# Counting edges per node: a loop of comparisons and matmuls written out for all hundred groups, its line numbers compared in four pieces, with four buffers in place of two

## The reference, cut to what matters

```
x = _layernorm(x + _L0_gnn_ref(x, edge_attr_48, src, dst, L0_gnn_eps), axis=-1)
x = _layernorm(x + _L1_gnn_ref(x, edge_weight, src, dst), axis=-1)
x = _layernorm(x + _L2_gnn_ref(x, edge_weight1, L2_gnn_weight1, L2_gnn_weight2, L2_gnn_bias1, L2_gnn_bias2, src, dst, edge_type_8), axis=-1)
x = _layernorm(x + _L3_gnn_ref(x, L3_gnn_theta_w, L3_gnn_theta_b, L3_gnn_phi_w, L3_gnn_phi_b, src, dst), axis=-1)
```

## Time and profile before

| | us |
|---|---|
| median of 3 runs | 4202.54 |
| lowest and highest of them | 4201.44, 4211.9 |
| span of the profiled execution | 5230.0 |
| counting stage in it, first compare to last result | 51.7 to 416.1 |

### The profile page before, as it was taken

How to read it: one execution, slowest core, us unless ns; L and a number is a source line. 1 busy time by engine, 2 the same in 40 slices (tenths; PEclk the granted TensorE clock), 3 DMA queues, 4 the chain that set the end, 5 groups by cost and what they waited for, 6 DMA issues and landing times. The chain is left out here.

```text
span 5230.0 us, 57991 instructions
## 1 busy us (share of the span) xinstructions
PE 2653.0 (51%) x9282; PEld 1302.4 (25%) x9282; DVE 2825.2 (54%) x7308; ACT 1341.5 (26%) x4703; POOL 2738.0 (52%) x2688
## 2 busy tenths in 40 slices
PE   1270000566666665357543577767666103975543
PEld 0150000232222233112111234433333001332222
DVE  3298998566666454356432366656665223652322
ACT  0003333344333232112111233333332011431111
POOL 4406773554454455544365355555556555646565
PEclk7695555777777777678776688877887556995555
DMA  7705777555555442334422544444443243321111
GB/s 249 295 0 164 217 216 198 140 146 144 140 142 134 141 115 78 86 99 114 93 55 52 123 116 113 110 102 106 101 102 77 64 125 91 73 63 31 30 30 22
DMA packets 513328, 587.96 MB, mean 112 GB/s; under 512 B 222598, under 2 KB 402382, under 8 KB 508182
## 3 DMA queue, kind: packets, MB, share of 16 engines
q1 hardware_dynamic: 365050, 417.75, 26.1%
q0 software_dynamic: 92160, 94.65, 11.9%
q10 hardware_dynamic: 55972, 74.03, 4.4%
HBM read 289.08 MB, written 303.60 MB: 113 GB/s over the span
## 5 line engine op out<-in xcount | busy, mean ns | idle before, releaser
L508 POOL DMA_INDIRECT xdst<-in_x,dstc x400 | 447.1, 1118 | 385.0 <-PEq L667 198.6
L284 POOL DMA_INDIRECT gb<-nodes,ib x400 | 386.1, 965 | 460.4 <-ACT ib L873 338.5
L268 PE MATMUL bank<-ident,act 128*99 128x128 f32 x400 | 87.4, 357 | 642.5 <-issue 570.5
L278 PE MATMUL bank<-ident,scan 99*128 99x99 f32 (+2 forms) x1120 | 205.6, 313 | 376.8 <-DVE scan L1032 139.8
L1314 PE MATMUL bank<-e_bxT,w 105*128 105x512 f32 x432 | 252.9, 702 | 224.7 <-ACT e_hm L1233 173.1
L304 PE MATMUL bank<-chosen,rec 128*6 128x512 bf16 x1200 | 360.8, 464 | 1.1 <-ACT packed L901 0.8
L1265 POOL DMA_INDIRECT out<-e_xob,e_ob x288 | 295.5, 1026 | 101.3 <-issue 86.8
L278 PEld LDWEIGHTS bank<-ident,scan 99*128 99x128 f32 (+2 forms) x1120 | 159.3, 213 | 560.5 <-issue 559.8
L284 POOL DMA_INDIRECT ugb<-nodes,ib x160 | 170.0, 1062 | 240.5 <-ACT ib L1984 158.5
L586 PE MATMUL bank<-hot_at,hot_no 128*125 128x400 f16 x800 | 167.9, 357 | 235.1 <-DVE hot_at L612 138.0
L284 POOL DMA_INDIRECT parent<-upper_rows,ib x160 | 159.3, 996 | 197.1 <-ACT ib L1544 148.2
(11 more groups left out here) (332 smaller groups left out, 7175.9 us busy)
## 6 DMA issues: line engine op xcount, KB each, us to landing
nodes<-wt SPq DMA_DIRECT2D x40, 1286.2 KB
lone_rows<-gb ACTq DMA_DIRECT2D x100, 294.0 KB
e_lsb<-lone_rows SPq DMA_DIRECT2D x72, 294.0 KB
parents<-zeros SPq DMA_DIRECT2D x21, 960.0 KB
upper_rows<-tb SPq DMA_DIRECT2D x100, 194.0 KB
deep_sum<-zeros SPq DMA_DIRECT2D x20, 960.0 KB
layer<-zeros SPq DMA_DIRECT2D x20, 960.0 KB
kb<-edge_keep SPq DMA_DIRECT2D x100, 192.0 KB
```

The source lines that it names most:

```text
L268: last = nc.tensor.transpose(slot(dst_ps[0:w, :], t), rows_sb[:, t, c0:c0 + w], ident[:, :])
L278: last = nc.tensor.transpose(dst_ps[:, t, 0:w], slot(cols_sb[0:w, :], t), ident[0:w, 0:w])
L284: yield nc.gpsimd.indirect_dma_start(out=dst[s][:, t, 0:width], out_offset=None, in_=table, in_offset=bass.IndirectOffsetOnAxis(ap=ib[s][: ...
L508: nc.gpsimd.indirect_dma_start(out=xdst[:, k * F:(k + 1) * F], out_offset=None, in_=a["x"], in_offset=bass.IndirectOffsetOnAxis(ap=dstc[:, ...
```

## The change

In `compare`, the one `tensor_tensor` over 512 columns becomes four `tensor_scalar` over 128 columns, each with its line number read per partition, and they alternate with the four of `hot_at`. Both read their number straight from `line_no` and `line_at`. The tile `marks`, ACT's copies and the semaphore `s_mark` go. The loops of DVE and PE are written out for all hundred groups, with constants in the place of registers. There are AHEAD = 4 buffers of the one-hots in place of two; the compare of group g now waits for PE to be through with group g - 4.

```diff
@@ buffers @@
-            hot_no = [sc(f"hot_no{b}", [P, T, P], F16) for b in range(2)]
-            hot_at = [sc(f"hot_at{b}", [P, T, LINE], F16) for b in range(2)]
-            marks = [sc(f"marks{b}", [P, T]) for b in range(2)]
+            hot_no = [sc(f"hot_no{b}", [P, T, P], F16) for b in range(AHEAD)]
+            hot_at = [sc(f"hot_at{b}", [P, T, LINE], F16) for b in range(AHEAD)]
@@ scalar @@
-                    def mark(i, b):
-                        g = i * 2 + b
-                        wait(act, s_hots, g - 1)
-                        nc.scalar.copy(marks[b][:, :], col(line_at, g)).then_inc(s_mark, 1)
...
@@ tensor @@
-                    def add(i, b, first=False, final=False):
-                        pe.wait_ge(s_hots, i * 2 + b + 1)
+                    def add(g, first=False, final=False):
+                        b = g % AHEAD
+                        pe.wait_ge(s_hots, g + 1)
                         pe.sem_inc(pe_turn, 1)
...
-                    with pe.Fori(1, NG // 2 - 1) as i:
-                        for b in range(2):
-                            add(i, b)
...
+                    for g in range(NG):
+                        add(g, first=g == 0, final=g == NG - 1)
@@ vector @@
-                    def compare(i, b):
-                        g = i * 2 + b
-                        wait(dve, s_count, g - 1)
-                        nc.vector.tensor_tensor(hot_no[b][:, :, :], steps_h[:, 0:P].unsqueeze(1).to_broadcast([P, T, P]), col(line_no, g).unsqueeze(2).to_broadcast([P, T, P]), ALU.is_equal)
-                        dve.wait_ge(s_mark, g + 1)
+                    def compare(g):
+                        b = g % AHEAD
+                        wait(dve, s_count, g - AHEAD + 1)
                         for t in range(T):
-                            last = nc.vector.tensor_scalar(hot_at[b][:, t, :], steps_h[:, :], marks[b][:, t:t + 1], None, ALU.is_equal)
+                            k = g * T + t
+                            nc.vector.tensor_scalar(hot_no[b][:, t, :], steps_h[:, 0:P], line_no[:, k:k + 1], None, ALU.is_equal)
+                            last = nc.vector.tensor_scalar(hot_at[b][:, t, :], steps_h[:, :], line_at[:, k:k + 1], None, ALU.is_equal)
                         last.then_inc(s_hots, 1)
...
-                    with dve.Fori(2, NG // 2) as i:
-                        for b in range(2):
-                            compare(i, b)
+                    for g in range(NG):
+                        compare(g)
```

More of the change, by code:

```diff
@@ L31 @@
 EARLY = 32
+AHEAD = 4
 FIRST = 7
@@ L526, in gnn @@
             s_fixed, s_term = scope.sem("h_fixed"), scope.sem("h_term")
-            s_zeros, s_fill, s_list, s_ends, s_endc, s_mark, s_hots, s_count, s_upto, s_below, s_fin, s_turn = (
-                scope.sem(f"h_{n}") for n in ("zeros", "fill", "list", "ends", "endc", "mark", "hots", "count", "upto",
+            s_zeros, s_fill, s_list, s_ends, s_endc, s_hots, s_count, s_upto, s_below, s_fin, s_turn = (
+                scope.sem(f"h_{n}") for n in ("zeros", "fill", "list", "ends", "endc", "hots", "count", "upto",
                                               "below", "fin", "turn"))
@@ L564, in _ @@
                 def _(act):
-                    def mark(i, b):
-                        g = i * 2 + b
-                        wait(act, s_hots, g - 1)
-                        nc.scalar.copy(marks[b][:, :], col(line_at, g)).then_inc(s_mark, 1)
-                    for i in range(2):
-                        for b in range(2):
-                            mark(i, b)
-                    with act.Fori(2, NG // 2) as i:
-                        for b in range(2):
-                            mark(i, b)
                     act.wait_ge(s_endc, 16)
@@ L588, in add @@
                         last.then_inc(s_count, 1)
-                    add(0, 0, first=True)
-                    add(0, 1)
-                    with pe.Fori(1, NG // 2 - 1) as i:
-                        for b in range(2):
-                            add(i, b)
-                    add(NG // 2 - 1, 0)
-                    add(NG // 2 - 1, 1, final=True)
+                    for g in range(NG):
+                        add(g, first=g == 0, final=g == NG - 1)
                     pe.wait_ge(s_upto, 2)
```

## The result

The changed kernel takes 4217.1 us (median of 5 runs, 4213.82 to 4220.78), the kernel before 4202.54 (4200.3 to 4211.9). The ratio is 1.003 with a 95% interval of 1.0017 to 1.0043: slower by 7 to 18 us, which lies around the bound that I had set for what a measurement can tell from no change. The forecast was 4208.0.

A forecast was written before the change was run, and what follows sets the result against it. The prediction took DVE to bound the counting stage, at 1.95 us a group without late increments. Short comparisons add 5.5 us, copies, loops and four buffers nothing: 4202.5 + 5.5 = 4208.0 us, range 4150 to 4255.

The forecast's parts named there:

- within 0.3%: Whole kernel: a time of 4190 to 4215 us, about what a measurement can't tell from no change; chance 0.65.
- main term: DVE's counting stage: four short comparisons for one wide add 0.055 us a group, +5.5 us over a hundred groups.
- late increments: DVE's waits for PE's semaphore in the counting stage, 152.9 us: taken for a cost of profiling, absent from timed runs.
- B: Counting stage: stalls real, from loops or register waits; vanishing gives 4054 us (0.06), two cases within 0.3% have 0.07.
- The line numbers: DVE's comparisons: 0.167 us for each of 128 columns, so 2.01 us a group for 1.95.
- bounds of -22 and +31 us: Short comparisons on DVE: -22 us if their fixed part were half as long, +31 if not overlapped at all.
- Rival D: POOL's gathers lengthened by DVE's comparisons, 1.89 for 0.94 us: slower, 4279 us; chance 0.03.
- The copies: ACT's hundred copies of 0.19 us lie wholly under DVE's compares: removing them gains nothing.
- The loops: DVE's and PE's loops: removing branch and registers gives nothing where DVE is the bound; gain 0.
- rival C: Written out code fetched while fills own the DMA engines: six holes on DVE, 46 us, 4254 us; chance 0.09.
- rival A: Counting stage: increments late by a small L without profiler too; four buffers cover about 4.3 us; 4157 us, chance 0.13.
- Four buffers: One-hot buffers between DVE and PE: nothing gained, as PE is 0.3 us early already with two.

The follow-up runs named there:

- pe_loop: The kernel after, with PE's code a loop of four groups again; DVE stays written out, with four pieces and four buffers: 4216.04 us (1.0029).
- loop_wide_dve_out: Against the kernel before: DVE written out, no number copies, four buffers; PE in a loop, one wide comparison of 512 columns: 4203.52 us (0.9998).
- loop_pieces: The kernel before, loops and two buffers kept, line numbers compared in four pieces of 128 columns and copied by ACT too: 4212.35 us (1.0018).
- two_slots: The kernel after, with two buffers in place of four: 4230.57 us (1.0067).
- one_wide: The kernel after, with the line numbers compared by one instruction of 512 columns as before: 4209.76 us (1.0013).
- act_half: From the kernel before: loops of four groups, four buffers, ACT makes two of four `hot_no` columns, DVE compares the other two: 4171.1 us (0.9925).

## Why the prediction was right, and where it was wrong

The time came out 9 us above the forecast, inside the range of 4150 to 4255. The forecast's own range, 4199 to 4213, to which I had given 0.58, it misses by 4 us, and the median lies 2 us above the end of the case "within 0.3%" (4215), while the ratio, 1.003 with 1.0017 to 1.0043, leaves both sides of that bound open. The mechanism of the main term was right. But of 11.7 us of stage I had seen 5.5. That the rest is so small is in part luck: with two buffers PE's holes take 19 us, the four buffers hold back 15 of them, and I had worked out neither number.

| part | forecast | by the stage | from |
|---|---|---|---|
| pieces, start-up | +5.5 | +5 | 2.00 against 1.95 us, no gathers |
| pieces, beside POOL's gathers | 0 | +3.6 to +4.1 | pe_loop, loop_wide_dve_out, loop_pieces |
| PE written out | 0 | +3.7 | after less pe_loop |
| DVE written out, copies gone, four buffers | 0 | -1.1 | loop_wide_dve_out less before |
| together | +5.5 | +11.7 | after less before |

**Whether the late increments exist without the profiler.** Right, and everything hung on it. I had forecast a stage from 51.7 us to 247 for the last compare and a tail of 15 us; the kernel before, run again, has its last comparison at 250.3 (a group takes 1.98 us and not 1.95 beside POOL). Of the reasons, the balance of 1027.5 us between span and median was sound. The cause that I named, the recording of PE's many instructions, was not shown: nine further profiled executions, with the same 9282 matmuls and mostly the same fills, have no such wait. I had taken a mishap of one execution for a property of profiling, and so forecast "the same gaps" and a span of 5230 for the profile after. That was wrong. So was the test that I set myself: "if those gaps are gone from the profile, B holds and I am wrong by 150 us". They are gone, and B (loops or register waits cause them) is false, since they are gone from the unchanged kernel too. A test on the changed kernel alone could not tell these apart.

**The line numbers.** The line through the 800 and 512 columns gave 0.167 us from start to start and 2.01 us a group; measured are 0.16 and 2.00. (4 x 0.167 less 0.61 is 0.058 and not 0.055, so by its own numbers the sum was +5.8.) The bounds of -22 and +31 us were not needed. What failed is the step from the group to the hundred: both durations came from stretches in which POOL gathers nothing (beside the rows from 961.57 to 962.62 it waits for ACT until 962.63), and I used them for a stage of which four fifths run beside 128 gathers. Rival D looked at this same encounter from POOL's side only, and gave little to it, rightly: POOL's gathers are not long enough to matter. The price was on DVE's side, 0.05 us for each gather where it had been 0.02.

The start-up of some 158 cycles of the Trainium skill ("VectorE: DVE Perf Modes", section "Side-by-side"), with which I had worked out +9 us, comes close to the total of the pieces (8.6 and 9.1) by accident: the part without gathers is 5.

**The copies.** Right, zero: with them and without, DVE stands for nothing (loop_pieces, pe_loop).

**The loops.** On DVE right, zero both ways. On PE wrong. I had the case in rival C, with its sign to be seen in the profile ("gaps in the middle of a group, before an instruction with no wait"), and that is what stands there. But I priced it for DVE, where there is no such hole, with POOL's hole of 7.59 us as the price, and waved PE's away: "a hole in PE's code would be bridged by four buffers". Bridged it was, by three quarters. What was missing is the lead to weigh a hole against. I had written that the wait for PE "is met 6 us ahead". In the kernel after PE is through with one group at 137.40 us and the comparison that needs its buffer starts at 141.85: 4.45 us ahead, close to the 4.3 that I had given for L in rival A. The hole of 4.4 us and the matmuls at the lower clock behind it make the group in which they stand 5.7 us late, so the buffers don't cover it, and some 1.3 us a hole reach DVE. PE then makes up its arrears with 0.46 us a group. Measured: 3.7 us for three long holes and a short one, and 15.4 more with two buffers.

POOL's hole of 7.59 us, my price for C, stands in the kernel before and after at the same gather; it has to do with neither of the parts that are changed. With the fills later it stands behind the same gather, the 113th, but is 3.30 us long, so full DMA engines lengthen it too; they run at full strength in the eight other profiled executions, where it is 7.3 to 8.2 us. What it is stays open.

**Four buffers.** "Nothing" was right for the stage as I saw it (1.1 us at its start, no more), and wrong for the kernel that they came with, where they hold back 15 us. The slack with two buffers, "0.3 us", is 301.57 - 301.40 = 0.17 us by the earlier trace rows; that changes nothing here.

**A, B and D.** A would have shown a median of 4140 to 4185: in the nine other profiled executions no comparison waits for a late increment. B in all its forms falls with it. D's deciding point was 1.63 us for each gather; they take 1.28 with their issue.

The unit in which code comes is told by the queue: five packets of 16 KB in this stage, one for fifteen groups of PE (the rows under pe_loop). In "Runtime: NRT & Kernel Launch", section "Instruction fetch mechanics", the Trainium skill gives blocks of 256 instructions as the unit of fetching, and holds the cost of crossing into the next to be mostly hidden. The unit agrees: a group of PE is 8 weight loads, 8 matmuls and one increment, 17 instructions, so that 256 hold 120.5 matmuls, and the holes stand 121, 120 and 121 matmuls apart. The cost does not: with the DMA engines at 403 GB/s one block in fifteen groups held PE for 4.3 to 4.5 us, with them at 20 GB/s for 0.7 to 0.9. And a loop, which it would have avoided, cost nothing here.

## What to carry to other kernels

Before anything rests on a wait that makes one profiled execution much longer than the timed runs, take the profile of the unchanged kernel again: it cost one run and would have replaced the most uncertain argument of this prediction. Writing out a loop makes its code a DMA transfer, which here came late when the DMA engines were full; leave PE in its loop there, and count the slower matmuls behind a hole with the hole. DVE written out cost nothing. Before trusting buffers to bridge a hole, take the lead that they give from the rows (4.45 us) and compare it with the whole delay of the group (5.7). And where DVE is the bound, cutting one instruction into four paid start-up four times, and more for each encounter with POOL; moving half of it to an idle engine gained 30.4 us of stage where the whole change had lost 11.7.

## What the runs showed of the hardware that I had not expected

- Increments of semaphores behind PE's work came up to 40 us late in one profiled execution (span 5230.0 us), and in none of nine others, eight of which had the fills at 403 to 404 GB/s where it had 402. The cause was not found.
- PE's code arrives in packets of 16 KB, one for fifteen groups of this stage. Four of the five in it go with a hole of PE's, and PE goes on 2.2 to 2.5 us behind the packet (2.8 once, in two_slots). The holes are 4.3 to 5.3 us long with full DMA engines (after, two_slots, one_wide) and 0.7 to 0.9 with nearly idle ones. DVE's code arrives in 8 KB packets and delays nothing that shows, under the same load.
- Behind a hole of 4.4 us PE's granted clock was 0.50 and a matmul of 400 columns took 0.35 us, against 0.19 ahead of it. Behind a hole of 0.9 us the granted clock was 1.00 and a matmul took 0.18.
- An indirect DMA issued by POOL costs DVE about 0.02 us in the kernel before, 0.05 us where half of DVE's instructions are short, and nothing in act_half; POOL's gathers start every 1.32, 1.28 and 1.36 us in the same three, so where DVE pays less, POOL pays more.
- POOL stands for 7.3 to 8.2 us behind the 113th gather with full DMA engines, and for 3.3 us with nearly idle ones. The cause was not found.
